# A landmark-attention and mixture-of-experts layer in FP32: first stage rewritten, small similarities moved into the value stage, 71 expert tiles in place of 72

## The reference

```python
q_l = q.reshape(b, H, M, l, DH).sum(axis=3) / l        # and k_l
attn1 = softmax(q @ k_l.T);  attn2 = softmax(q_l @ k_l.T);  attn3 = softmax(q_l @ k.T)
out = attn1 @ moore_penrose_inverse(attn2) @ (attn3 @ v)
out = out + depthwise_conv(out, 13 taps along the sequence)
x = x + (out @ w_fc + b_fc)                            # attention on layernorm(x)
```

## Time and profile before

| | us |
|---|---|
| median of 3 runs (1268.49 to 1276.77) | 1270.55 |
| the profiled execution | 1270.24 |
| its span, first to last instruction | 1268.5 |
| PE busy in it | 1180.4 |

### The profile page before, as it was taken

The page is one execution under the profiler, slowest core; times in us unless marked ns, Lnnn a source line. Parts: engine busy times, 40 slices in busy tenths (PEclk is TensorE's granted clock), DMA queues, the critical chain, the costliest instruction groups (busy, mean ns, idle before and its releaser), DMA issues.

```text
span 1268.5 us, 26553 instructions
## 1 busy us (share of the span) xinstructions
PE 1180.4 (93%) x10452; PEld 974.9 (77%) x10452; DVE 629.1 (50%) x1334; ACT 306.2 (24%) x522; POOL 299.5 (24%) x242
## 2 busy tenths in 40 slices
PE   4989989999998889999999999939999999999997
PEld 4876767777678775676777667728999999999996
DVE  7472222222224655657667767673444444444442
ACT  1332222222222332333233332311111111111111
POOL 3000000000001000323454345442422232223332
PEclk9889999999999999999999999868999999999999
DMA  4720010101003004021132221242232232222220
GB/s 141 292 108 1 23 46 0 67 0 41 26 0 101 5 4 154 18 94 59 61 133 76 83 86 60 84 143 56 48 50 48 44 51 46 49 44 48 48 42 10
DMA packets 50424, 78.90 MB, mean 62 GB/s; under 512 B 8592, under 2 KB 42640, under 8 KB 48016
## 3 DMA queue, kind: packets, MB, share of 16 engines
q1 hardware_dynamic: 35728, 55.65, 13.5%
q0 software_dynamic: 13440, 16.93, 7.7%
q10 hardware_dynamic: 1152, 4.86, 1.0%
HBM read 46.59 MB, written 27.67 MB: 59 GB/s over the span
## 4 chain that ended last, share of the span: by engine, by line
PE 90%; DVE 4%; issue 3%; ACT 1%; DMA 1%; POOL 1%; POOLq 0%; SPq 0%; DVEq 0%; ACTq 0%
PE ps L1396 20%; PE ps L1406 10%; PE ps L1164 10%; PE ps L1298 9%; PE ps L1117 9%; PE ps L1337 8%; PE ps L1329 5%; PE ps L1150 2%; PE ps L1211 2%; PE ps L1074 2%; PE ps L1136 1%; PE ps L1089 1%; PE ps L1317 1%; PE ps L1390 1%; PE ps L1283 1%
## 5 line engine op out<-in xcount | busy, mean ns | idle before, releaser
L1396 PEld LDWEIGHTS ps<-mem 128*128 128x128 f32 x2304 | 270.6, 193 | 4.6 <-DVE mem L1039 0.9
L1396 PE MATMUL ps<-mem 128*128 128x128 f32 x2304 | 271.1, 276 | 0.6 <-ACT mem L682 0.6
L511 POOL DMA_INDIRECT out<-mem x72 | 127.4, 1769 | 282.9 <-DVE mem L1033 192.3
L1406 PE MATMUL ps<-mem 128*128 x576 | 136.4, 380 | 0.9 <-DVE mem L1052 0.9
L1298 PE MATMUL ps<-mem 128*128 128x512 f32 x288 | 129.7, 594 | 1.3 <-DVE mem L842 1.3
L466 POOL TENSOR_TENSOR mem<-mem,small 128x1024 f32<-128x1024 f32 x36 | 68.5, 1904 | 257.3 <-DVE small L958 124.4
L1164 PE MATMUL ps<-mem 128*128 128x128 f32 x1024 | 122.6, 278 | 5.6 <-DVE mem L791 5.6
L1164 PEld LDWEIGHTS ps<-mem 128*128 128x128 f32 x1024 | 116.8, 192 | 8.4 <-issue 4.4
L690 ACT ACTIVATE mem<-ps 128x512 f32<-128x512 f32 x72 | 43.0, 597 | 331.3 <-PE ps L1396 331.3
L1337 PE MATMUL ps<-mem 128*128 128x256 f32 x512 | 120.8, 390 | 0.0
L1117 PE MATMUL ps<-mem 128*128 128x512 f32 x256 | 114.8, 593 | 5.2 <-ACT mem L565 5.2
(11 more groups left out here) (203 smaller groups left out, 1418.5 us busy)
## 6 DMA issues: line engine op xcount, KB each, us to landing
mem<-xs_d SPq DMA_DIRECT2D x72, 130.0 KB, 2.1
mem<-xnt_d SPq DMA_DIRECT2D x8, 1056.0 KB, 5.0
mem<-w_gu SPq DMA_DIRECT2D x8, 1024.0 KB, 6.9
xnt_d<-mem ACTq DMA_DIRECT2D x4, 1056.0 KB, 5.8
mem<-x SPq DMA_DIRECT2D x8, 512.0 KB, 5.4
mem<-mem SPq DMA_DIRECT2D x4, 1024.0 KB, 4.7
mem<-x SPq DMA_DIRECT2D x32, 128.0 KB, 2.2
out<-mem SPq DMA_DIRECT2D x32, 128.0 KB, 1.7
```

What stands on the lines that cost most here:

```text
L511: pool.indirect_dma_start(out=out_rows, out_offset=bass.IndirectOffsetOnAxis(ap=xs[:, v, D + 1:D + 2].bitcast(U32), axis=0), in_=ys[:, v], ...
L1396: mm = pe.matmul(bank(2 * c + u)[:, f * P:(f + 1) * P], wgu[:, u, k, c, f * P:(f + 1) * P], xst[:, u, k], start=(k == 0), stop=(k == KD - 1))
L1406: mm = pe.matmul(bank(4 + u)[:, 0:D], hid[:, u, f * P:(f + 1) * P], w_d_s[:, e, f], start=(f == 0), stop=(f == 3))
```

## The change

Four parts:

1. **First stage.** All of x, and then the weights of queries and keys, of values and of the output side of queries, are loaded without a wait. DVE does the statistics of batch b + 1 before it normalises batch b; the Newton steps move to POOL; ACT normalises 3 of 8 row tiles. PE multiplies each block once with `ids`, a unit matrix and the 8 summing columns side by side (136 moving columns, a matmul and no transpose), in chunks of 3, 3 and 2 row tiles through all 8 banks; ACT takes each product apart into `xnts[b]` and `xm`. The four batches have a buffer each, so nothing is read back from DRAM in the value stage.
2. **Landmarks.** `q_p` and `k_p` are plain copies, one by ACT and one by DVE for each pair, and the block-diagonal forms and their POOL memsets are gone; `g3` is formed for all batches at once, in 8 rounds of 4 matmuls on 64 rows with 256 moving columns, copied half by ACT and half by DVE.
3. **Value stage.** No hardware loop; the 32 head pairs are written out, two to a turn. The small similarities of all batches (64 matmuls of 64 x 64 in place of 32 of 128 x 64) and the transposes of the softmax stand in the first four turns. `e3t` has two buffers; `utb` and the value product take two head pairs at a time, while the row sums stay at 16 matmuls of 128 moving columns for each head pair. POOL writes the unit start value of the inverse (`w_of`) after the first products of the inverse, no longer before the value stage.
4. **Experts.** NTILE is 71; the tables keep 72 entries (NTAB).

```diff
-NTILE += -NTILE % RING
+NTILE = (2 * TOK + E * (P - 1)) // P
+NTAB = NTILE + -NTILE % RING
...
-STARTED = (
-    "a_xnt", "a_lm", "a_xnt_out0", "a_xnt_out1",
-    "c1_sim", "c1_exp", "c1_tp", "c1_e3a", "c1_e3b", "c1_ut", "c1_utb", "c1_v3mm", "c1_v3",
-)
+CHUNKS = ((0, 1, 2), (3, 4, 5), (6, 7))
+ACT_ROWS = (2, 5, 7)
+NP2 = NQ // 2
...
-            for name in STARTED:
-                sp.sem_inc(s(name), 1)
-
             for b in range(B):
-                if b >= 2:
-                    sp.wait_ge(s("a_xn"), RT * (b - 1))
                 for hf in range(2):
                     ts = slice(RT // 2 * hf, RT // 2 * (hf + 1))
-                    sp.dma_start(xbs[:, b % 2, ts], x_t[b, :, ts]).then_inc(s(f"a_x_in{b % 2}{hf}"), 16)
+                    sp.dma_start(xbs[b][:, ts], x_t[b, :, ts]).then_inc(s(f"a_x_in{b}{hf}"), 16)
             sp.dma_start(wqk, w_qkv[:, 0:2 * INNER].rearrange("(k p) c -> p k c", p=P)).then_inc(s("w_qk_in"), 16)
-
-            sp.wait_ge(s("a_xnt"), 1 + 4 * B)
-            sp.dma_start(wkt, wk_t.rearrange("(j p) c -> p j c", p=P)).then_inc(s("w_in"), 16)
-            sp.dma_start(wv, w_qkv[:, 2 * INNER:].rearrange("(k p) c -> p k c", p=P)).then_inc(s("w_in"), 16)
+            sp.dma_start(wkt, wk_t.rearrange("(j p) c -> p j c", p=P)).then_inc(s("w_k_in"), 16)
+            sp.dma_start(wv, w_qkv[:, 2 * INNER:].rearrange("(k p) c -> p k c", p=P)).then_inc(s("w_v_in"), 16)
...
+            sp.wait_ge(s("a_xn_dve"), (RT - len(ACT_ROWS)) * (B - 1))
+            sp.wait_ge(s("a_xn_act"), len(ACT_ROWS) * (B - 1))
+            sp.dma_start(wfc, w_fc.rearrange("(j p) c -> p j c", p=P)).then_inc(s("w_in"), 16)
...
-            for u in range(2):
-                sp.wait_ge(s(f"a_xnt_out{u}"), 1 + 16 * B // 2)
-
-            with sp.Fori(0, B) as b:
-                sp.wait_ge(s("c1_sim"), 1 + J * b)
-                sp.dma_start(xnt, xnt_d[b].rearrange("p (k n) -> p k n", k=KD)).then_inc(s("c1_xnt_in"), 16)
-                sp.wait_ge(s("c1_ut"), 1 + J * b)
-                sp.dma_start(xnb, xna[:, b]).then_inc(s("c1_xn_in"), 16)
...
-            sp.wait_ge(s("c1_sim"), 1 + J * B)
-            batch_columns(0)
-            sp.wait_ge(s("b_sim2"), B)
+            sp.wait_ge(s("c1_sim"), NQ)
             sp.dma_start(band, conv_band.rearrange("h p c -> p h c")).then_inc(s("band_in"), 16)
-            sp.wait_ge(s("c1_v3mm"), 1 + NQ)
-            batch_columns(1)
...
+            for b in range(B):
+                pool.wait_ge(s("a_guess"), b + 1)
+                r, w = rs[:, b], tmp[:, b]
+                for _ in range(3):
+                    ch.link(pool.tensor_tensor(w, r, r, ALU.mult))
+                    ch.link(pool.tensor_tensor(w, w, ve[:, b], ALU.mult))
+                    ch.link(pool.tensor_scalar(w, w, -0.5, 1.5, ALU.mult, ALU.add))
+                    ch.link(pool.tensor_tensor(r, r, w, ALU.mult))
+                ch.link(pool.tensor_tensor(w, mv[:, b, :, 0], r, ALU.mult))
+                pool.tensor_scalar(nb[:, b], w, -1.0, 0.0, ALU.mult, ALU.add).then_inc(s("a_rs"), 1)
...
-            pool.wait_ge(s("b_lm"), 2 * J)
+            pool.wait_ge(s("c1_ut"), NQ)
+            pool.wait_ge(s("i_y0mm"), 4)
             pool.tensor_scalar(w_of, eye1.unsqueeze(1).to_broadcast([P, NQ, M]), 1.0, 0.0, ALU.mult, ALU.add)\
...
+            def normalise(b):
+                act.wait_ge(s("a_rs"), b + 1)
+                for t in ACT_ROWS:
+                    act.activation(xna[:, b, t], xbs[b][:, t], ACT.Identity, bias=nb[:, b, t:t + 1], scale=rs[:, b, t:t + 1])\
+                       .then_inc(s("a_xn_act"), 1)
...
+            def columns_out(b):
+                for n, ts in enumerate(CHUNKS):
+                    for k in range(KD):
+                        c = 6 * b + 2 * n + k
+                        act.wait_ge(s("a_tp"), c + 1)
+                        product = bank(c % 8)[:, 0:len(ts) * (P + RT)].rearrange("p (t c) -> p t c", t=len(ts))
+                        at_ = HALO + P * ts[0]
+                        act.activation(xnts[b][:, k, at_:at_ + P * len(ts)].rearrange("p (t c) -> p t c", t=len(ts)),
+                                       product[:, :, 0:P], ACT.Copy).then_inc(s("a_xnt"), 1)
...
+                if b >= 1:
+                    act.wait_ge(s("a_xnt"), 12 * (b + 1))
+                    act.dma_start(xnt_d[b].rearrange("p (k n) -> p k n", k=KD), xnts[b]).then_inc(s("a_xnt_out"), 16)
+
+            for b in range(B):
+                normalise(b)
+                columns_out(b)
...
+                act.activation(q_p[:, j], bank(2 * j % 8)[:, 0:B * M], ACT.Copy, scale=DH ** -0.5 / (N // M))\
+                   .then_inc(s("b_q"), 1)
+
+            for n in range(2 * KD * 2):
+                k, j = n // 4, 2 * (n % 4)
+                act.wait_ge(s("c1_g3mm"), n + 1)
+                for i in range(2):
+                    act.activation(g3[:, :, k, 2 * (j + i)], bank(2 * (n % 4))[:, 256 * i:256 * i + 256].rearrange("p (b c) -> p b c", b=B),
+                                   ACT.Copy).then_inc(s("c1_g3a"), 1)
...
+            c1_exp(0)
+            c1_exp(1)
+            for m in range(NP2):
+                c1_e3(2 * m)
+                if m < 2:
+                    sim2_exp(2 * m)
+                    sim2_exp(2 * m + 1)
...
+                c1_e3(2 * m + 1)
+                for n in (2 * m + 2, 2 * m + 3):
+                    if n < NQ:
+                        c1_exp(n)
+                act.wait_ge(s("c1_ut"), 2 * m + 2)
+                if m >= 1:
+                    act.wait_ge(s("c1_v3mm"), m)
+                act.activation(utb, bank(6).rearrange("p (k c) -> p k c", k=KD), ACT.Copy).then_inc(s("c1_utb"), 1)
...
+            row_statistics(0)
+            for b in range(1, B):
+                row_statistics(b)
+                normalise(b - 1)
+            normalise(B - 1)
...
-                for half in range(2):
-                    pe.wait_ge(s("a_xnt"), 1 + 4 * b)
-                    pe.wait_ge(s("a_lm"), 1 + b)
-                    for t in range(4):
-                        pe.wait_ge(s("a_xn"), RT * b + 4 * half + t + 1)
-                        for k in range(KD):
-                            mm = pe.transpose(bank(2 * half + k)[:, t * P:(t + 1) * P],
-                                              xna[:, b, 4 * half + t, k * P:(k + 1) * P], idt)
-                    mm.then_inc(s("a_tp"), 1)
-                for t in range(RT):
+                for n, ts in enumerate(CHUNKS):
+                    pe.wait_ge(s("a_xn_dve"), (RT - len(ACT_ROWS)) * b + sum(t not in ACT_ROWS and t <= ts[-1] for t in range(RT)))
+                    pe.wait_ge(s("a_xn_act"), len(ACT_ROWS) * b + sum(t <= ts[-1] for t in ACT_ROWS))
                     for k in range(KD):
-                        mm = pe.matmul(bank(4)[:, k * M + RT * t:k * M + RT * (t + 1)], xna[:, b, t, k * P:(k + 1) * P],
-                                       sums16[:, :], start=True, stop=True)
-                mm.then_inc(s("a_lmmm"), 1)
...
+                        c = 6 * b + 2 * n + k
+                        if c >= 8:
+                            pe.wait_ge(s("a_xnt"), 2 * (c - 7))
+                        for i, t in enumerate(ts):
+                            mm = pe.matmul(bank(c % 8)[:, i * (P + RT):(i + 1) * (P + RT)], xna[:, b, t, k * P:(k + 1) * P],
+                                           ids[:, :], start=True, stop=True)
+                        mm.then_inc(s("a_tp"), 1)
...
-            for g in range(B):
-                for j in range(J):
-                    mm = pe.matmul(bank(g)[:, j * M:(j + 1) * M], q_bd[:, j, g], k_st[:, j, g], start=True, stop=True)
-                mm.then_inc(s("b_sim2"), 1)
...
+            pe.wait_ge(s("w_k_in"), 16)
+            for n in range(2 * KD * 2):
+                k, j = n // 4, 2 * (n % 4)
+                if n < 4:
+                    pe.wait_ge(s("b_q"), 5 + n)
+                    pe.wait_ge(s("b_k"), 5 + n)
+                else:
+                    pe.wait_ge(s("c1_g3a"), 2 * (n - 3))
+                    pe.wait_ge(s("c1_g3b"), 2 * (n - 3))
+                for i in range(2):
+                    for h, r in enumerate(halves):
+                        mm = pe.matmul(bank(2 * (n % 4) + h)[:, 256 * i:256 * i + 256], wkt[r, j + i, k * P:(k + 1) * P],
+                                       q_p[r, j + i], start=True, stop=True)
+                mm.then_inc(s("c1_g3mm"), 1)
+
+            def c1_sim(n):
+                b, j, u = n // J, n % J, n % 2
+                if n >= 2:
+                    pe.wait_ge(s("c1_exp"), n - 1)
...
+            def c1_tp(n):
+                pe.wait_ge(s("c1_exp"), n + 1)
+                if n >= 1:
+                    pe.wait_ge(s("c1_e3a"), n)
+                    pe.wait_ge(s("c1_e3b"), n)
+                for t in range(RT):
+                    mm = pe.transpose(bank(4 + t // 4)[:, (t % 4) * P:(t % 4 + 1) * P], ex[:, n % 2, t * P:(t + 1) * P], idt)
+                mm.then_inc(s("c1_tp"), 1)
+
```

(53 more changed lines are left out.)

429 lines of the change are left out of this document (187 added, 242 removed).

## The result

The changed kernel takes 1206.28 us (median of 4 runs, 1204.51 to 1208.99) against 1272.14 of the kernel before beside it: a ratio of 0.948 (0.944 to 0.952). Forecast were 1220 and a range from 1208 to 1236. So the direction was right and the gain, 65.9 us against 50.5, was larger than the range allows, by 1.7 us. The kernel before, measured beside each, stood higher too (1274.97 and 1272.75), so that the three gains are 65.9, 63.7 and 62.7 us, where the low end of the range, 1208 against 1270.55, stood for 62.6.

What follows compares the result with a forecast made beforehand. PE, busy for 93%, was taken to bound the kernel; 28.9 us less before the similarities, 16.1 in the value stage and 5.5 in the experts sum to 50.5, giving 1220 us, range 1208 to 1236.

Steps and rivals of the forecast that it cites:

- every cover worked out for the waits in the pair: Value stage: other PE work hides each wait, such as 4.2 us against 0.7 for the copies of banks 4 and 5.
- the cost of the small products: Value stage: 64 small products and 64 transposes added to the head pairs' 270.4 us, at 7.9 us.
- the tile: Experts: one tile less, at 5.52 us from tile to tile, makes the kernel 5.5 us shorter.
- B: Value stage: a wait in the pair isn't covered or a list is badly ordered; stage keeps 296, kernel 1236; chance 0.05.
- C: Value stage: written-out instructions must be brought in, 4.6 us a turn, 1294 us, or near no change; chance 0.04.
- The later write of `w_of`: Inverse: POOL is ready 6 us after its start, the first reader comes at 9.6; cost 0, at most 1 us.
- The loss of up to 1.5 us a batch: First stage: DVE operations may wait for POOL's Newton steps, putting DVE at 7.0 us a batch, 3 us in all.
- The start of the similarities: End of first stage, landmarks and `g3`: first similarities at about 67 us instead of 95.86, 28.9 us less.
- Between these I take one batch at the lower level (8.6 us): First stage: between no further low-clock batch and three, one batch takes 8.6 us; the stage ends at 43.
- 5.0 of ACT, plus PE's first group (0.7), plus handing over (0.3), 6.0 us: First stage: each batch is this chain set by ACT, with DVE hidden; three more batches at 6.0 us.
- `g3`: After the landmarks: 8 rounds of 0.94 us plus 0.3, 7.8 us, with the copies hidden behind the next round.
- What is paired (`utb`, the value product) saves no matmul. So 270.4: Value stage: 32 head pairs stay at 8.45 us each, 270.4 us, within a stage of 280.0 against 296.1.

Runs made afterwards that it cites:

- the first profile: Profile from the first of three measurements of the unaltered changed kernel: 1206.28 us, ratio 0.948 to the kernel before; the repeats took 1211.32 and 1210.05 us.

## Why the prediction was right, and where it was too small

**What held.** PE bounds the kernel throughout; the value stage's head pairs follow without a gap; every cover worked out for the waits in the pair held, and the cost of the small products nearly did (a turn with them takes 18.73 us, 2.2 more than 16.53: 8.8 over four turns, forecast 7.9); the tile is 5.5. Rivals B and C didn't come about: 0.3 us in all of waiting for the copies of banks 4 and 5, no "issue" before L1158 or L1138. The later write of `w_of` cost nothing, as forecast: POOL ends it at 340.19, 6.0 us after the inverse's first product, and the first product that reads it (L1273) starts at 343.00. The loss of up to 1.5 us a batch that DVE might have beside POOL's Newton steps didn't come either: its five rows took 1.70 or 1.71 us in each batch, and it was POOL's steps beside them that took up to 0.29 us instead of 0.20.

**The start of the similarities, 59.0 instead of 67 (forecast ends 62 to 73).** Three terms make up 7.7 of the 8 us. The first is the step "Between these I take one batch at the lower level (8.6 us)": it never came. After 19.2 us the clock stayed up, though PE paused for 1.1 to 1.6 us before each batch. That is 2.6 us in the first stage, and 2.0 in the landmarks, which took 14.0, the figure that I had for a full clock, and not 15.5 with 0.5 before. I had leaned on the earlier trace rows, pauses between 64-column products, which are another kind of work. The prediction also named the Trainium skill, TensorE: Matmul & The Clock Gate (A second HAM failure mode: psum-queue depth-cycling), where short pauses between groups make the clock swing. That didn't happen here: the banks are cycled, the pauses are there, and the stage ended at 37.9 at the full clock, not at 49. The experiments show what I had not asked: the kernel before ran at the lower level up to 41.8 us while PE was nearly always busy (one pause of 0.52 us a batch), and the run of identity products with separate sums stayed there through 9.6 us without any pause, so the pauses were not the cause. It could be read in the earlier trace rows: 32 short sums took 6.83 us without a pause between them, and 3.95 later. Giving them back their separate place costs 18.7 us at the start (77.50 against 58.81), half of all that the start gained. Most of that is the clock: at the higher level the separate sums were estimated at 5.7 us of PE a batch ahead of that run, near the period of 5.55, and the batches came every 9.8 to 10.3. The prediction had counted the merging only as fewer matmuls.

The second is the period, "5.0 of ACT, plus PE's first group (0.7), plus handing over (0.3), 6.0 us", charged for each of three batches. It measured 5.55 twice, and by another chain than this one. Lines of ACT in the changed kernel, one batch (L521 rows, L531 and L534 copies):

```profile
27.18 1.58 ACT L521 ACTIVATE mem<-mem 128x256 f32<-128x256 f32 x3 [0.43 <-ACT mem L534]
28.84 0.49 ACT L531 ACTIVATE mem<-ps 128x384 f32<-128x384 f32 x1
...
29.54 0.49 ACT L531 ACTIVATE mem<-ps 128x384 f32<-128x384 f32 x1
...
31.86 0.39 ACT L531 ACTIVATE mem<-ps 128x256 f32<-128x256 f32 x1
...
32.72 1.58 ACT L521 ACTIVATE mem<-mem 128x256 f32<-128x256 f32 x3 [0.41 <-ACT mem L534]
```

PE starts at 27.87, 0.69 us after ACT begins its three rows and as soon as the first is there, not behind all of them; its 16 products take 3.94, and a pair of ACT's copies follows every 0.70, which is the pace of three products; the last copies and the send come 0.9 behind PE. Together these are the 5.55. PE's own products stand in that chain, and ACT, which waits for them between its pairs of copies, isn't the list that sets it. The last batch has no successor to wait for, so the landmarks start 4.49 after its start. The two periods and the end give 0.9 and 1.5 us. The third is `g3`, 7.1 instead of 7.8: 0.89 a round, not 0.94.

**The value stage, 275.1 instead of 280.0.** The failing step is "What is paired (`utb`, the value product) saves no matmul. So 270.4". It saves none, but it saves one of two visits in a turn, and a visit costs 0.34 us beyond its matmuls. Sixteen turns at 16.53 are 264.5; the forecast's 270.4 is 5.9 too much, and the run with two visits gives back 5.4. The remainder, 10.6 against 9.6 forecast for small products and ends, goes the other way. The trace of before held the price: L1164 starts 0.15 us after the last value product and not 0.11, and its first records are further apart.

**The range.** Its low end allowed 5 us at the start and 7 in the stage. The misses were 8 and 5, of one sign, and the remaining 1.7 us in the first profile lies within the output stage's spread. A low end with some 3 us more, for the stages that the change leaves alone, would have held, but by luck: the start was 3 us outside its own bound.

## What to carry to other kernels

Few-column products are not cheap for what they hold: let them ride as extra columns of a wide product with the same weights, and check the record lengths, since a stage with a busy PE can run at half speed from end to end. Count visits as well as matmuls where small tiles alternate with large ones. Work out a period as one chain, from an engine's first result to the next engine's start, and not as the sum of a whole list and what stands beside it; and charge it between batches, not ahead of the first nor behind the last.

## What was unexpected of the hardware

- TensorE stayed at the lower level for 42.5 and 64.4 us with 8-column products between 128-column ones, busy for 34.67 of 39.50 and 55.12 of 60.00 us, and left it 3.9 us after the first 136-column product.
- A change from 64-column products to 128-column work and back costs 0.34 us a visit without a wait between them.
- A DVE operation with two SBUF operands took 2.20 us instead of 0.68 beside POOL's addition, one with a PSUM operand its usual 0.69.
- In three profiles of the same kernel inverse and output stage differ by 2.2 and 4.2 us, more than two of the edits tried here are worth; the value stage repeats within 0.01. In these three the output stage is the longer, the more of it passes at 0.50 (24.3, 30.4 and 36.5 us).
